# A two-layer attention and expert kernel on one core: layer 1's result is written into the output, and layer 2's product is added to it there by accumulating DMAs

## The reference

```python
x = L0_attn_x
xn = _layernorm(x)
s = _L0_attn_ref(xn, ...)              # latent attention, 32 heads
g = _silu(_L0_ffn_ref(xn, ...))        # dense product with low-rank experts
x = x + s * g                          # "layer 1's result" below
xn = _layernorm(x)
s = _L1_attn_ref(xn)                   # attention across the batch
g = _silu(_L1_ffn_ref(xn, ...))        # 8 experts, top 2 of each row
x = x + s * g
return x
```

## Time and profile before

| what | us |
|---|---|
| device time, three runs | 1470.6, 1473.92, 1482.49 |
| median | 1473.92 |
| device time of the profiled execution | 1472.43 |
| its span, first to last instruction | 1470.6 |
| last matmul starts | 1434.78 |
| last VectorE instruction starts | 1467.44 |

### The profile page before, as it was taken

How to read it: one execution, slowest core, us unless ns; L and a number is a source line. 1 busy time by engine, 2 the same in 40 slices (tenths; PEclk the granted TensorE clock), 3 DMA queues, 4 the chain that set the end, 5 groups by cost and what they waited for, 6 DMA issues and landing times. The chain is left out here.

```text
span 1470.6 us, 25078 instructions
## 1 busy us (share of the span) xinstructions
PE 1342.6 (91%) x7870; PEld 1146.6 (78%) x7871; DVE 702.0 (48%) x1636; ACT 566.5 (39%) x1775; POOL 606.9 (41%) x510
## 2 busy tenths in 40 slices
PE   6989899999999999999977579999999999999990
PEld 6934478878787878788746469999999999999980
DVE  6362376767666666676846342322222232222228
ACT  4431276665665555556644221221212112121224
POOL 0020154455444545454524627071735344472412
PEclk9899999999999999999987689999999999999995
DMA  9035790000000000000013657182846455582547
GB/s 294 2 86 145 269 384 18 15 15 14 15 14 14 14 14 14 14 14 15 23 59 109 242 182 243 52 268 78 295 166 202 161 185 188 158 293 65 186 138 278
DMA packets 73229, 181.72 MB, mean 124 GB/s; under 512 B 6592, under 2 KB 15184, under 8 KB 72864
## 3 DMA queue, kind: packets, MB, share of 16 engines
q0 software_dynamic: 24624, 94.53, 19.2%
q1 hardware_dynamic: 42944, 76.39, 15.9%
q10 hardware_dynamic: 5616, 10.23, 2.0%
HBM read 125.28 MB, written 55.84 MB: 123 GB/s over the span
## 5 line engine op out<-in xcount | busy, mean ns | idle before, releaser
L1834 PE MATMUL bank<-expert_weights,rows_t 128*128 x1872 | 359.2, 347 | 2.2 <-DVE rows_t L1748 1.6
L1834 PEld LDWEIGHTS bank<-expert_weights,rows_t 128*128 128x128 f32 x1872 | 340.7, 189 | 6.1 <-issue 3.0
L991 ACT ACTIVATE room<-bank,room 128x256 f32<-128x256 f32 (+1 forms) x512 | 209.3, 416 | 115.4 <-DVE room L904 115.3
L1019 POOL TENSOR_TENSOR room<-room 128x1024 f32<-128x1024 f32 (+1 forms) x128 | 188.1, 1470 | 119.4 <-DVE room L881 119.4
L1760 DVE TENSOR_TENSOR x_keep<-x_keep,bank 128x400 f32<-128x400 f32 x78 | 44.5, 571 | 304.5 <-ACT x_keep L1691 303.1
L755 PE MATMUL bank<-room 96*128 (+2 forms) x1024 | 188.9, 327 | 0.0
L1135 POOL TENSOR_TENSOR expert_weights<-x_keep,expert_weights 128x1600 fp32r<-128x1600 f32 (+2 forms) x49 | 160.3, 3271 | 53.5 <-DMA expert_weights<-w 53.1
L755 PEld LDWEIGHTS bank<-room 96*128 96x128 f32 x1024 | 159.0, 191 | 13.7
L1857 PE MATMUL bank<-expert_weights,act_t 128*128 x702 | 165.6, 389 | 1.0 <-ACT act_t L1696 1.0
L1030 POOL TENSOR_TENSOR room<-room 128x256 f32<-128x256 f32 x128 | 93.3, 729 | 170.9 <-DVE room L965 169.7
L1691 ACT ACTIVATE x_keep<-bank 128x400 f32<-128x400 f32 x78 | 39.4, 505 | 296.8 <-PE bank L1834 291.3
(11 more groups left out here) (251 smaller groups left out, 1765.3 us busy)
## 6 DMA issues: line engine op xcount, KB each, us to landing
x_keep<-w POOLq DMA_DIRECT2D x28, 800.0 KB, 4.9
expert_weights<-w POOLq DMA_DIRECT2D x28, 800.0 KB, 6.7
x_keep<-w POOLq DMA_DIRECT2D x14, 768.0 KB, 5.2
expert_weights<-w POOLq DMA_DIRECT2D x14, 768.0 KB, 6.9
rows_by_expert<-room SPq DMA_DIRECT2D x1, 9984.0 KB, 29.7
results_by_row<-room SPq DMA_DIRECT2D x1, 9984.0 KB, 55.5
x_keep<-rows_by_expert SPq DMA_DIRECT2D x39, 256.0 KB
results_by_row<-x_keep ACTq DMA_DIRECT2D x39, 256.0 KB, 5.0
```

The costliest lines, as they stand in the source:

```text
L991: last = sc.activation(Pr[:, m % 4, hh, 0:w], scores_bank(m)[:, w * hh:w * hh + w], ACT.Exp, bias=nb[:, par, hh:hh + 1], accum_out=sm[:, p ...
L1019: g.tensor_tensor(pr, pr, rs[:, one[1] % 2].unsqueeze(2).broadcast_to([P, 4, w]), ALU.mult).then_inc(normed, 1)
L1834: last = mm(psum(2 * hf + w)[:, 0:HF], xgT[:, par, of_x, P * k:P * k + P], W[:, ds(off + (of_w * SLOT + (k * 2 + w) * FF + hf * HF), HF)], ...
```

## The change

Layer 1's result is stored straight into `out` in `attention`, and the internal tensor is gone. At the end VectorE no longer adds it, SyncE no longer brings it back, and the product `z[:, t]` goes to `out` by a DMA of GpSimd that adds it to what lies there (`accum_op=ALU.add`). These sixteen DMAs stand behind all gathers in GpSimd's program. SyncE only waits for them. `done` now counts one for each tile.

```diff
-        s.x1 = nc.dram_tensor("x_after_layer1", [NB * SEQ, D], F32, kind="Internal").ap()
...
-                sp.dma_start(s.x1[ds(t * P, P), :], X[:, ds(t, 1)].rearrange("p t n -> p (t n)")).then_inc(
+                sp.dma_start(s.out[ds(t * P, P), :], X[:, ds(t, 1)].rearrange("p t n -> p (t n)")).then_inc(
                     s.x1_stored, 16)
...
-    x1_at = [xg[:, 1]] + in_tiles(act_.rearrange("p i n -> p (i n)"))
-    X1 = len(x1_at)
-    x1_at += higher[:NT - X1]
...
                 bring_rows(higher[t], t, 1, higher_in[t])
 
+
+            for t in range(NT):
+                pool.wait_ge(done, t + 1)
+                pool.dma_start(s.out[P * t:P * t + P, :], z[:, t], accum_op=ALU.add).then_inc(stored, 16)
+
...
-            def bring_x1(t):
-                sp.dma_start(x1_at[t], s.x1[P * t:P * t + P, :]).then_inc(x1_in[t % X1], 16)
-
-            sp.wait_ge(x_turned, NBLK)
-            bring_x1(0)
-            sp.wait_ge(a_turned, NBLK)
-            for t in range(1, X1):
-                bring_x1(t)
-            for t in range(NT):
-                if t + X1 < NT:
-                    sp.wait_ge(summed, t + 1)
-                    sp.wait_ge(x1_in[t % X1], 16 * (t // X1 + 1))
-                    bring_x1(t + X1)
-                sp.wait_ge(done, 2 * t + 2)
-                sp.dma_start(s.out[P * t:P * t + P, :], z[:, t]).then_inc(stored, 16)
             sp.wait_ge(y_in0, 16 + 16 * (NBLK // 2 + 1))
             sp.wait_ge(y_in1, 16 + 16 * (NBLK // 2))
             sp.wait_ge(stored, 16 * NT)
...
                 v.tensor_tensor(z[:, t], z[:, t], S[:, t], ALU.mult).then_inc(done, 1)
-                dve.wait_ge(done, 2 * t + 1)
-                dve.wait_ge(x1_in[t % X1], 16 * (t // X1 + 1))
-                v.tensor_tensor(z[:, t], z[:, t], x1_at[t], ALU.add).then_inc(done, 1)
```

More of the change, by code:

```diff
@@ L1561, in experts @@
     higher_in = [sem(f"higher_in{t}") for t in range(NT)]
-    x1_in = [sem(f"x1_in{i}") for i in range(X1)]
     SCALED_FIRST, BESIDE_LAST = 6, 6
@@ L1598, in _ @@
             pool.wait_ge(first_w2, NCH - KT_PER_D - 1)
-            for stored in s.messages_stored:
-                pool.wait_ge(stored, 16)
+            for kept in s.messages_stored:
+                pool.wait_ge(kept, 16)
             bring_high(0)
```

## The result

The change makes the kernel slower by 0.4%, which is little but clear of the spread: the median is 1484.93 us (1479.28 to 1492.95, 20 runs) against 1479.16 us before, measured beside it (20 runs), a ratio of 1.0041 with a 95% interval of 1.0024 to 1.0058. The forecast was a ratio of 1.0004, nearly no change, and a range that holds the result. The loss is 6 us and not 0.6. On the forecast's own base of 1473.92 us the measured ratio makes 1480.0 us, just above the 1470 to 1479 that it gave its likeliest case.

What follows compares the result with a forecast made beforehand. TensorE was busy 1342.6 of 1470.6 us and VectorE set the end; with the change, first accumulation at 1448.5, transfers 20.7 and landing 2.0 gave 1471.2, or 1474.5 against the median, range 1464 to 1492.

Steps and rivals of the forecast that it cites:

- likeliest case: Whole kernel: the forecast itself, accumulations costing a load and a store each; 1470 to 1479 us, chance 0.45.
- VectorE: After the last matmul: without sums a round takes 1.33 us in place of 1.99, VectorE ends 10.6 us earlier.
- GpSimd's order: GpSimd's queue at the end: last gather ends at 1447.7, then sixteen issues of 0.777 us each, until 1460.1.
- The accumulating transfers: DMA engines at the end: each tile costs a load and a store, 1.3 us at 405 GB/s; sixteen take 20.7 us.
- The estimate of 248 GB/s: Accumulating transfers: rate for sixteen DMA engines from the skill page, 17 us in place of 20.7, span some 4 us shorter.
- B: Accumulating transfers: cost hardly more than a store, 10.4 us; span 7.8 us below now, 1466.1 on the median; chance 0.23.
- C: Accumulating transfers: read, addition and write run one after the other; at the upper bound 30.7 us more, 1504.6; chance 0.20.
- D: GpSimd's queue: issuing accumulations sets the end; at twice a gather's 1.26 us, 20.4 us more, 1494.3; chance 0.08.
- First accumulation issued at 1447.7 + 0.3 + 0.5 = 1448.5; 20.7 us of transfers: Behind the last gather: accumulations start at 1448.5 and their transfers end at 1469.2.
- 1471.2. That is the span: Last step of the sum: 2.0 us for landing behind 1469.2, then the span ends, 0.6 us above 1470.6.
- the store to another address: Store of layer 1's result: same instruction on the same queue to another address, costed at nothing.

Runs made afterwards that it cites:

- e3: The change with plain stores of the product by SyncE, layer 1's result not added; last matmul to end 24.5 us, against 35.8 before and 41.8 in the change.
- e7: The change with eight accumulating DMAs of two tiles each in place of sixteen; last matmul to end 41.2 us, against 41.8.
- e11: The change with SyncE's pairs of load and plain store for accumulations, started about where the last gather is issued, nothing added; last matmul to end 38.5 us.
- e2: The change with GpSimd's sixteen DMAs storing plainly, layer 1's result not added; last matmul to end 31.3 us, against 41.8.
- e9: SyncE stores the product plainly as in e3, but GpSimd stores the last tile, nothing added; last matmul to end 28.3 us, against 24.5.
- e1: The kernel before with only the place of layer 1's result moved to the output; last matmul to end 35.8 us, ratio 1.0005.
- e5: Tiles 4 to 11 accumulated by GpSimd behind the gathers, the others summed by VectorE as before; last matmul to end 33.7 us, ratio to before 0.9984.
- e10: As e11, but the pairs of load and plain store started 11 us too early, ahead of the last ten gathers; last matmul to end 32.8 us.
- e8: As e5, but only six tiles (4 to 9) accumulated by GpSimd; last matmul to end 33.3 us, ratio to before 0.9979.
- e6: The kernel before with GpSimd itself adding layer 1's result for tiles 6 to 14, no accumulating DMA; last matmul to end 41.2 us, ratio 1.0041.
- e4: The change with accumulations placed among the gathers from tile 8's gather on; last matmul to end 41.1 us, ratio to before 1.0025.
- e12: As e5, but tiles 2 to 9 accumulated, six of them between the last gathers; last matmul to end 34.7 us, ratio to before 0.9996.

## Why the prediction was right, and where its size was off

**VectorE.** The forecast was 1.33 us a round and the last product done at +22.7; it is 1.26 and +21.9. The earlier trace rows had the better number: the 0.61 us from the sum to the next add_higher, where nobody waits for the sum, and 0.66 give 1.27. e3 shows that its gain would have been 11.3 us had nothing followed. That it would be covered wholly by the transfers was right.

**GpSimd's order.** The last gather was to end at +12.9 and ended at +13.1. The issues were taken at 0.777 us and are 0.90. They were covered, as forecast: in e7 they take some 4 us less and the end moves by 0.6 us.

**The accumulating transfers.** The main term, a load and a store for a tile at 405 GB/s, 1.3 us, is right: 1.30 us at a full share, and e11, with real pairs, lands its last store at the same +38.3. The Trainium skill's rule from the page "Collectives: The Full Stack", section "The bandwidth ceiling: the fold count and why AG ≠ RS ≠ AR" (an addition in the DMA gives half a copy's rate), came out in the ratio, 202 to 405. The estimate of 248 GB/s that the prediction worked out from the page's figure was too high for this kernel. Rivals B, C and D are out: e2 is what B describes, and it ends 10.5 us earlier than the change; C wanted over 30 us of transfers at a share well below 1, and they took 25.2 us at a share of 1.1; e7 excludes D.

The term that was off by a little is "First accumulation issued at 1447.7 + 0.3 + 0.5 = 1448.5; 20.7 us of transfers". The forecast has the last landing at +36.4 and it is at +38.3: 25.2 us behind the first issue in place of 22.7, with the first issue itself 0.6 us earlier than forecast. The rows show two pieces. From 1452 to 1456 the rate was 155 GB/s and not 202, which is worth 0.9 us; why it is lower there I didn't find. And the last gather's rows were still on their way, to about 1452.6, when the first accumulations were issued (share 0.81 from 1450 to 1452, full only from 1452 on); the rest of the 2.5 us, 1.6, would be this slow start, which no run shows by itself.

**The end of the program.** The step of the sum that failed is its last: "1471.2. That is the span", with nothing behind the last landing. It holds for a kernel whose last DMA is SyncE's. With GpSimd's the wait at the barrier is 3.2 us in place of 0.2, and e9 brings the same about with a single DMA. This is the larger part of the miss: between the forecast +36.4 and the measured +41.8 lie 5.4 us, of which 3.5 stand behind the last landing (3.2 of them the wait at the barrier) and 1.9 are the transfers.

**The rest.** I had put the store to another address at nothing; e1, e3 and e5 show no cost. The 7.8 us between the two spans thus are 6.0 of the end, and 1.9 by which executions differ anyway. The medians say 5.8. That the result fell into the range says little by itself, since the range went from 10 us faster to 18 us slower; what the runs bear out is the main term.

The change loses because it takes 11 us from the engine that set the end, and puts behind GpSimd's last gather 20.7 us of DMA time, of which the old order had spent five loads (3.2 us) ahead of the end and much of the rest beside the gathers. e10 shows the price of the late start: the same plain pairs, begun 11 us earlier, end 5.7 us earlier.

**What beats both** is e8, by 2.5 us in the end and 0.2% in the ratio (some 0.6% against the change, if the two ratios are divided, 1.0041 / 0.9979): six sums taken off VectorE, in the stretch where GpSimd is done with its gathers and before SyncE's last stores. As it is the best of several variants and its interval ends at 0.9997, the gain over the kernel before is a thin one.

## What to carry to other kernels

An accumulating DMA frees the engine that added, but not the DMA engines, which carry a load and a store for it; before moving a sum there, ask whether they have that time, and from which point on. Move so many tiles that both ends meet, rather than all. And if a few microseconds count, let SyncE issue the last DMAs and GpSimd be done early: here the program ended no sooner than 3.1 us after GpSimd's last DMA landed, and 5.4 us after its last sum (e6).

## What the runs showed of the hardware

- Where a DMA of GpSimd lands last, the wait at the closing barrier is 2.9 to 3.5 us (e2, e4, e7, e9 and the change), accumulating or not; where it is one of SyncE and GpSimd has long been done, 0.2 us (before, e1, e3, e10, e11). From the latest landing of GpSimd's last DMA to the end of the program it is 3.1 to 3.8 us (e2, e4, e5, e7, e8, e9, e12 and the change).
- An accumulating DMA moves 202 GB/s of result at a full DMA share, where loads and stores together move 390 to 405.
- Issued by GpSimd, a plain store of 128 rows of 2 KB takes 0.54 us and an accumulating one 0.90 on the mean (the change; 0.85 for a single one in e5).
- VectorE's product of 512 columns takes 0.68 us alone and 1.75 beside a sum of GpSimd, which takes 1.71.
- A semaphore instruction of GpSimd without a wait of its own, written behind ten gathers, let SyncE's load be issued before the first of them.
